# Deformable convolution of one fused kernel: row-tiled spreading of the sample points, 64-row products, three taps a multiply

## The reference, cut to what matters

```
def _dcnv4(t, H, W, Wv, bv, Wom, bom, Wo):     # N=8 images, 16x16 pixels, C=32, G=4 groups of Cg=8, K=9 taps
    value = (t @ Wv + bv).reshape(N, H, W, G, Cg)
    om = (t @ Wom + bom).reshape(N, H, W, G, 3 * K)
    offset = om[..., :2 * K].reshape(N, H, W, G, K, 2)
    mask = om[..., 2 * K:]
    loc_y = ys + ky + offset[..., 1]
    loc_x = xs + kx + offset[..., 0]
    sampled = _bilinear_gather(value, loc_y, loc_x)      # zero outside the image
    out = (sampled * mask[..., None]).sum(axis=4)
    return out.reshape(N, L, C) @ Wo
```

## Time and profile before

| what | value |
|---|---|
| median of three runs | 520.41 us (519.21 to 521.89) |
| the profiled execution | 518.91 us, its span 517.1 us |
| mean granted clock of TensorE | 0.952 of full speed |
| busy: PE / PEld / DVE / ACT / POOL | 463.7 / 325.7 / 419.9 / 302.2 / 212.5 us |
| instructions: PE / DVE / ACT / POOL | 3334 / 998 / 554 / 168 |

### The profile page before, as it was taken

The page is one execution under the profiler, slowest core; times in us unless marked ns, Lnnn a source line. Parts: engine busy times, 40 slices in busy tenths (PEclk is TensorE's granted clock), DMA queues, the critical chain, the costliest instruction groups (busy, mean ns, idle before and its releaser), DMA issues.

```text
span 517.1 us, 10243 instructions
## 1 busy us (share of the span) xinstructions
PE 463.7 (90%) x3334; PEld 325.7 (63%) x3334; DVE 419.9 (81%) x998; ACT 302.2 (58%) x554; POOL 212.5 (41%) x168
## 2 busy tenths in 40 slices
PE   6979889999987759999999859999999899699785
PEld 5868523333346637777778637877777888455474
DVE  4978899998783498999999598999998586799551
ACT  3742448898744347777771277777760223798540
POOL 4004450000000078999984189999974031000000
PEclk9999899999999678999999969999999999899995
DMA  8700000000000000000000000000000000000000
GB/s 325 329 2 0 1 1 1 1 1 0 1 1 1 0 2 1 1 0 0 1 0 1 1 1 1 0 1 0 0 1 0 1 1 1 2 1 2 2 1 20
DMA packets 1475, 9.16 MB, mean 18 GB/s; under 512 B 160, under 2 KB 928, under 8 KB 1056
## 3 DMA queue, kind: packets, MB, share of 16 engines
q1 hardware_dynamic: 1296, 8.62, 4.2%
q10 hardware_dynamic: 144, 0.07, 0.1%
HBM read 8.43 MB, written 0.26 MB: 17 GB/s over the span
## 4 chain that ended last, share of the span: by engine, by line
PE 60%; DVE 20%; ACT 8%; issue 6%; POOL 4%; DMA 0%; DVEq 0%; SPq 0%; POOLq 0%
PE bank L1226 24%; PE bank L1171 13%; PE bank L1207 6%; ACT RINGS L555 3%; DVE RINGS L780 2%; PE bank L985 2%; PE bank L1312 2%; PE bank L1292 2%; PE bank L1176 2%; DVE SMT L859 1%; DVE PRD L850 1%; POOL RINGS L255 1%; POOL PR L276 1%; DVE PR L692 1%; DVE XN L623 1%
## 5 line engine op out<-in xcount | busy, mean ns | idle before, releaser
L1226 PE MATMUL bank<-VB,RINGS 128*128 (+1 forms) x576 | 159.6, 415 | 0.3
L255 POOL TENSOR_TENSOR RINGS<-LXA,cst 128x1152 f32<-128x1152 f32 x32 | 69.2, 2162 | 125.8 <-DVE LXA L831 125.8
L1226 PEld LDWEIGHTS bank<-VB,RINGS 128*128 128x128 f32 x576 | 104.5, 195 | 23.0 <-issue 1.8
L850 DVE TENSOR_TENSOR PRD<-bank,HYM 128x288 f32<-128x288 f32 x288 | 110.6, 448 | 8.4 <-PE bank L1226 3.7
L780 DVE TENSOR_SCALAR RINGS<-XP,wb 128x512 f32<-128x512 f32 x176 | 79.4, 527 | 7.9 <-PE bank L1171 6.6
L460 ACT ACTIVATE RINGS<-XP,wb 128x512 f32<-128x512 f32 x112 | 70.1, 712 | 16.9 <-PE bank L1171 16.8
L985 PE MATMUL bank<-cst 128*128 128x128 f32 x650 | 78.6, 281 | 0.0
L985 PEld LDWEIGHTS bank<-cst 128*128 128x128 f32 x650 | 77.5, 198 | 0.5
L1171 PE MATMUL bank<-RINGS,cst 128*32 128x512 f32 x576 | 74.4, 598 | 3.7 <-DVE RINGS L780 3.7
L324 POOL TENSOR_TENSOR PRD<-PRD 128x864 f32<-128x864 f32 x32 | 65.2, 2038 | 17.5 <-DVE PRD L850 17.5
L859 DVE TENSOR_REDUCE SMT<-PRD 128x1728 f32 (+1 forms) x32 | 62.1, 1941 | 0.1
(11 more groups left out here) (247 smaller groups left out, 519.6 us busy)
## 6 DMA issues: line engine op xcount, KB each, us to landing
wb<-in_wb SPq DMA_DIRECT2D x1, 3068.5 KB, 12.3
wd<-in_wd SPq DMA_DIRECT2D x1, 2729.5 KB, 20.8
wc<-in_wc SPq DMA_DIRECT2D x1, 1255.0 KB, 14.9
cst<-in_cst SPq DMA_DIRECT2D x1, 645.0 KB, 5.4
XC<-in_x SPq DMA_DIRECT2D x2, 128.0 KB, 2.4
out_y<-XC SPq DMA_DIRECT2D x2, 128.0 KB, 1.8
wa<-in_wa SPq DMA_DIRECT2D x1, 209.0 KB, 5.5
cst<-in_cst ACTq DMA_DIRECT2D x1, 66.0 KB, 2.7
```

The costliest lines, as they stand in the source:

```text
L255: pool.tensor_tensor(view(DXY, o, [[WW, KG * NA], [1, WW]]), view(LXA, n * KG * NA, [[1, KG * NA], [0, WW]]), view(cst, CST["xg"], [[0, KG ...
L850: dve.tensor_tensor(view(PRD, (half * K9 + k) * 288, [[72, G], [NR, CG], [1, NR]]), view(bank[2 + (9 * half + k) % LOOK], 0, [[72, G], [NR ...
L1226: pe.matmul(bank[2 + (9 * half + k) % LOOK][:, 0:288], view(HXT, (half * K9 + k) * P, [[1, P]]), view(VB, b * 288, [[1, 288]]), start=True ...
```

## The change

The x hats are no longer made pixel by pixel and then turned. Instead the x locations themselves are turned, once an image (72 locations a pixel, laid out in three groups of 32 columns, 24 of them used: `turn_points`, 2 transposes). ACT copies them out (`points_out`). A matmul with a 0/1 matrix (`select`, a new constant of 384 columns) then repeats each location over 16 partitions: `spread(t)` is three matmuls, each contracting 32 rows at partitions 0, 32 and 64, into banks 4, 5 and 6, 256 columns (both halves) each. ACT takes |location - column| straight from these banks with the column as its bias (a new constant `mx`, one number a partition), three instructions of 256, and then relu(1 - .) on all 768 (`hats`). There are three such groups t an image, of three taps each. The banks are reused from one t to the next.

The y hats: POOL subtracts the rows for both halves (`rows_off`), ACT takes the absolute value and the relu on 648 elements (`rows_hat`), POOL multiplies by the mask (`masked`). HY holds them in place, in two buffers that alternate from image to image.

The products: for a half and three taps, six matmuls. Each contracts 64 rows (two groups) with 144 columns; the pair of one tap takes partitions 0 to 63 and 64 to 127 and writes different banks. DVE multiplies all three taps at once, 864 elements (`sample`); two pairs of banks alternate. POOL's `pairs` adds 864 elements as before, DVE's `sums` reduces 1728 as before. The channels come out in another order, for which the host permutes Wo. All loops over images are written out. Before the loop only image 0's points are finished; those of images 1 to 3 follow before the first multiply, those of images 4 to 7 are put into image 1. In PSUM, one tensor replaces the eight banks, with a small class that gives views.

The core of the diff (the old functions that it removes are in the code above):

```diff
+            def rows_off(turn, b):
+                i = B * turn + b
+                pool.wait_ge(lxa_ready, pointed(turn, b))
+                after(pool, prod_used, 6 * (i - 1))
+                for half in range(2):
+                    ins = pool.tensor_tensor(by_trio(HY, (b % 2 * 2 + half) * HYN), by_point(LY, 2 * b + half),
+                                             view(cst, CST["yg"], [[0, 3], [0, 3 * G], [1, NR]]), ALU.subtract)
+                ins.then_inc(dy_ready, 1)
+            def masked(turn, b):
+                pool.wait_ge(hy_ready, B * turn + b + 1)
...
+                for b in range(B):
+                    if b + 1 < B:
+                        rows_off(turn, b + 1)
+                    pairs(turn, b, 0)
+                    if b + 1 < B:
+                        masked(turn, b + 1)
+                    pairs(turn, b, 1)
...
+            def points_out(i):
+                act.wait_ge(t_done, i + 1)
+                after(act, sel_done, 9 * i)
+                act.activation(view(LXT, 0, [[1, NPIX]], n=LXW), bank[7][0:LXW, 0:NPIX], ACT.Copy).then_inc(lxt_ready, 1)
+            def rows_hat(i):
+                hy = view(HY, i % 2 * 2 * HYN, [[1, 2 * HYN]])
+                act.wait_ge(dy_ready, i + 1)
+                act.activation(hy, hy, ACT.Abs).then_inc(hy_abs, 1)
+                act.wait_ge(hy_abs, i + 1)
+                act.activation(hy, hy, ACT.Relu, scale=-1.0, bias=cv("one", 1)).then_inc(hy_ready, 1)
+            def hats(i, t):
+                after(act, prod_done, 6 * (i - 1))
+                hx = i % 2 * HXN + 3 * t * NPIX
+                for quad in range(3):
+                    act.wait_ge(sel_done, 9 * i + 3 * t + quad + 1)
+                    act.activation(view(HX, hx + quad * NPIX, [[1, NPIX]]), bank[4 + quad][:, 0:NPIX], ACT.Abs,
+                                   bias=cv("mx", 1)).then_inc(abs_done, 1)
+                act.wait_ge(abs_done, 9 * i + 3 * t + 3)
+                act.activation(view(HX, hx, [[1, 3 * NPIX]]), view(HX, hx, [[1, 3 * NPIX]]), ACT.Relu, scale=-1.0,
+                               bias=cv("one", 1)).then_inc(hat_ready, 1)
...
+                for b in range(B):
+                    i = B * turn + b
+                    points_out(i)
+                    rows_hat(i)
+                    for t in range(3):
+                        hats(i, t)
...
+            def sample(i, half, t):
+                q = 6 * i + 3 * half + t
+                dve.wait_ge(hym_ready, i + 1)
+                after(dve, smp_ready, 2 * i + half - 1)
+                after(dve, paired, 2 * i + half - 1)
+                dve.wait_ge(prod_done, q + 1)
+                dve.tensor_tensor(view(PRD, half * PRN + t * TRIO, [[3 * COLS, GP], [6 * NR, CG], [1, 6 * NR]]),
+                                  view(bank[q % 2 * 2], 0, [[512, GP], [6 * NR, CG], [1, 6 * NR]]),
+                                  view(HY, (i % 2 * 2 + half) * HYN + t * 3 * G * NR, [[6 * NR, GP], [0, CG], [1, 6 * NR]]),
+                                  ALU.mult).then_inc(prod_used, 1)
...
+                offsets(turn, 0, 0)
+                offsets(turn, 0, 1)
+                points(0, 1)
...
+                points(1, B4 - 1)
+                for b in range(B):
+                    i = B * turn + b
+                    sample(i, 0, 0)
+                    sample(i, 0, 1)
+                    if b:
+                        sums(i - 1, 1)
+                    sample(i, 0, 2)
+                    sample(i, 1, 0)
+                    sample(i, 1, 1)
+                    sums(i, 0)
+                    if b == 1:
+                        points(B4, B4)
+                    sample(i, 1, 2)
+                sums(B * turn + B - 1, 1)
...
+            def spread(turn, b, t):
+                i = B * turn + b
+                pe.wait_ge(lxt_ready, i + 1)
+                after(pe, abs_done, 9 * i + 3 * t)
+                for quad in range(3):
+                    pe.matmul(bank[4 + quad][:, 0:NPIX], cv("select", P, t * P, 32 * quad, 32),
+                              view(LXT, 0, [[1, NPIX]], 32 * quad, 32), start=True, stop=True).then_inc(sel_done, 1)
+            def products(turn, b, half, t):
+                i = B * turn + b
+                q = 6 * i + 3 * half + t
+                if half == 0:
+                    pe.wait_ge(hat_ready, 3 * i + t + 1)
...
+                after(pe, prod_used, q - 1)
+                for k3 in range(3):
+                    for gp in range(GP):
+                        ins = pe.matmul(view(bank[q % 2 * 2 + gp], k3 * NR, [[3 * NR, 2 * CG], [1, NR]]),
+                                        view(HX, b % 2 * HXN + (3 * t + k3) * NPIX + half * P, [[1, P]], 64 * gp, 64),
+                                        view(VB, b * COLS, [[NR, 2 * CG], [1, NR]], 64 * gp, 64),
+                                        start=True, stop=True, skip_group_check=True)
+                ins.then_inc(prod_done, 1)
...
+                for b in range(B):
+                    ahead = b + 1 < B
+                    if ahead:
+                        turn_points(turn, b + 1)
+                    for u in range(6):
+                        products(turn, b, *divmod(u, 3))
+                        if ahead and u in (0, 2, 4):
+                            spread(turn, b + 1, u // 2)
```

More of the change, by code:

```diff
@@ new lines, in masked, with pairs @@
+            def masked(turn, b):
+                pool.wait_ge(hy_ready, B * turn + b + 1)
+                for half in range(2):
+                    hy = by_trio(HY, (b % 2 * 2 + half) * HYN)
+                    ins = pool.tensor_tensor(hy, hy, by_point(MM, 2 * b + half), ALU.mult)
+                ins.then_inc(hym_ready, 1)
+            def pairs(turn, b, half):
+                i = B * turn + b
+                pool.wait_ge(prod_used, 6 * i + 3 * half + 2)
+                first, second = (view(PRD, half * PRN + t * TRIO, [[1, TRIO]]) for t in range(2))
+                pool.tensor_tensor(second, second, first, ALU.add).then_inc(paired, 1)
@@ L475, in _ @@
             norm(4, "eps6")
-            def absolute(turn, b, half):
-                n = 2 * b + half
-                o = half * HATS
-                act.wait_ge(dxy_ready, 16 * turn + n + 1)
-                act.activation(view(DXY, o, [[1, HATS]]), view(DXY, o, [[1, HATS]]), ACT.Abs).then_inc(abs_done, 1)
-            def hats(turn, b, half, begun=False):
-                n = 2 * b + half
-                o = half * HATS
-                if not begun:
-                    absolute(turn, b, half)
-                act.wait_ge(abs_done, 16 * turn + n + 1)
-                after(act, hx_turned, 3 * (16 * turn + n - 1))
-                after(act, hym_ready, 16 * turn + n - 1)
-                act.activation(view(HXY, o, [[1, HATS]]), view(DXY, o, [[1, HATS]]), ACT.Relu, scale=-1.0,
-                               bias=cv("one", 1)).then_inc(hxy_ready, 1)
@@ L507, in deform @@
                                    view(src, bh * NPIX, [[WW, NR], [7 * WW, NA], [1, WW]]), ACT.Copy).then_inc(xw_ready, 1)
-                hats(turn, 0, 0)
-                absolute(turn, 0, 1)
-                turned(turn, 0, 0)
-                hats(turn, 0, 1, begun=True)
-                def body(b, first=False):
-                    for half in range(2):
-                        if not (first and half == 0):
-                            turned(turn, b, half)
-                        hats(turn, b + 1, half)
-                body(0, first=True)
-                with act.Fori(1, B - 1) as b:
-                    body(b)
-                for half in range(2):
-                    turned(turn, B - 1, half)
+                for b in range(B):
[4 more added lines that the diff above has]
+                        hats(i, t)
                 act.wait_ge(smp_turned, turn + 1)
@@ L861, in sums @@
+            def sums(i, half):
+                bh, b4 = divmod(i % B, B4)
+                dve.wait_ge(prod_used, 6 * i + 3 * half + 3)
+                dve.wait_ge(paired, 2 * i + half + 1)
+                dve.tensor_reduce(view(SMT, bh * NPIX + half * P + b4 * C, [[1, C]]),
+                                  view(PRD, half * PRN + TRIO, [[3 * NR, C], [TRIO, 2], [1, 3 * NR]]), AX.XY,
                                   ALU.add).then_inc(smp_ready, 1)
             def deform(turn):
-                for half in range(2):
-                    offsets(turn, 0, half)
-                    points(half, 2, B4)
+                offsets(turn, 0, 0)
+                offsets(turn, 0, 1)
+                points(0, 1)
@@ L867, in deform @@
                 if turn == 0:
[L868 removed]
+                    dve.wait_ge(vb_clear, 2)
                 values(turn, 0)
[L870 to L872 removed]
                 values(turn, 1)
[L874 to L885 removed]
@@ L1241, in deform @@
                     ins.then_inc(val_done, 1)
-                turn_hats(turn, 0, 0)
-                def body(b, more, first=False):
-                    products(turn, b, 0, True, first)
```

(14 more changed lines are left out.)

237 lines of the change are left out of this document (80 added, 157 removed).

## The result

The changed kernel took 533.55 us (median of 4 runs, 530.22 to 535.55) against 521.07 (519.21 to 521.89, 4 runs) for the kernel before on the same chip: a ratio of 1.024, 95% interval 1.018 to 1.030. The forecast was 527, range 508 to 541, slower at 0.65. The profiled execution took 530.22 with a span of 528.4, and before 518.9 with 517.1: 11.3 us more. From the second copy of XNC to the end of the last reduction the first turn now takes 179.95 to 292.60 = 112.65 us, and the second, from the end of YC on, 110.93, where they took 106.1 and 106.2. That is 6.5 + 4.7 = 11.2 us, so all but 0.1 us of the difference lies in the two deformable turns.

What follows compares the result with a forecast made beforehand. PE bound the old loop, DVE hardly behind; a ring of waits would bind the new. A turn: 14.1 + 8 x 11.0 + 4.0 + 1.0 + 2.4 (clock) = 109.5, +3.4; two turns +6.8, so 525.7 profiled, 527 median, range 508 to 541.

Steps and rivals of the forecast that it cites:

- The ring: Deformable loop: waits from one image's last multiply through POOL, ACT, PE and DVE to the next image's, 11.0 us.
- Tile shape: PE, between spreads, products and transposes: each change of tile shape adds 0.09 us.
- rival 4: PE array empties at each tile-shape change: 0.17 at two changes in the ring, 0.34 an image, 532 us; chance 0.10.
- hand-overs between engines: In the ring: six passes from one engine to the next, about 0.05 us each, 0.3 together.
- 64-row tiles: Products on PE: pairs run side by side, 6 rounds of 144 columns at 0.122, 0.73 us a trio.
- Rival 3: Products on PE: 64-row tiles don't run side by side, a trio stays at 1.46 us, kernel 541; chance 0.08.
- Start of a turn: From XNC to the first product: 12.3 us at full clock, 14.1 with PE at 1.2 GHz, against 17.0 before.
- Points of images 4 to 7: Now between two multiplies of image 1: taken as 4.0 us a turn.
- The clock in the loop: PE clock falls in two images of eight, +1.2 us each, +2.4 a turn; bounds none to 14 us.
- the last reduction: End of a turn on DVE: 1.0 us added to the turn's sum.
- Rival 2: The ring stands but PE's clock holds in the loop: 522 us, 519 if also at the start; chance 0.26.
- Rival 1: Loop: ring hidden, DVE sets the pace, 9.6 + 0.3 us an image, a turn 98.3, kernel 505; chance 0.12.

Runs made afterwards that it cites:

- g3_shapes: e3_spread_later with the matmuls without a reader in a turn's tail replaced by 128-row, 32-row and alternating ones; 519.68 us in its only execution.
- k3_pool_adds_warm: g4_pool_adds plus 18 matmuls without a reader in the points' gap and three small ones in each image; 506.30 us, ratio 0.972 to the kernel before.
- e3_spread_later: The changed kernel with each spread put one product trio later on PE; 512.25 us, ratio 0.986 to the kernel before the change.
- g1_warm_ends: e3_spread_later plus matmuls without a reader behind a turn's first two spreads and in its last image; 504.85 us, ratio 0.968 to the kernel before.
- g4_pool_adds: e3_spread_later, third HY buffer, g1_warm_ends' matmuls; POOL adds one half's third trio, DVE reduces 864 elements there; 508.73 us, ratio 0.977 to the kernel before.

## Why the prediction was right, and which terms were off

**The ring: right, 0.11 short.** It was put at 11.0 us and measures 11.11. Multiply 1.06 (measured 1.05), distances 0.74 + 0.79 (1.46 for two), y hats to the first absolute value 1.53 (364.99 to 366.50, 1.51), three absolute values 1.21 (1.19), reduction 1.94: all within 0.07. The cause was put to the test on three engines, and each edit took it away.

**Tile shape: mechanism misread, effect small.** I took 0.09 a change and gave rival 4 a chance of 0.10. The timeline of PE in the kernel after shows more:

```profile
240.19 0.71 PE L1209 MATMUL bank<-RINGS,cst 32*128 32x256 f32 x6
240.83 1.01 PE L1224 MATMUL bank<-VB,RINGS 64*128 64x144 f32 x12
241.76 0.42 PE L1200 MATMUL bank<-cst,LXA 128*96 128x128 f32 x2
```

Two rounds of the spread are 0.43, but the next shape starts 0.64 after it; six product rounds are 0.73, and the transposes start 0.93 after: 0.2 us each, the same as in g3_shapes. The array empties before another shape starts, as the Trainium skill says (TensorEngine Tiling (Array Packing), Key Properties), and the trace agrees. My reading of the earlier trace rows was the error. A record of a matmul there starts before the one ahead of it ends, but I took that for work side by side; its own length holds the wait. In the ring one change counts, and 0.2 in place of 0.09 is 0.11 or so, as much as 11.11 exceeds 11.0 by. (The hand-overs between engines also came to some 0.45 in place of 0.3, and the shorter distances, y hats and absolute values made up for it.) Rival 4 had the mechanism, but it counted two changes in the ring at 0.17 more each, where the runs show one at 0.11 more.

**64-row tiles: right.** The records of a pair start 7 ns apart and the rounds of one trio 0.122, so six rounds are 0.73. Rival 3 is out.

**Start of a turn: right.** 14.1 forecast, 13.97 and 14.0 measured, with the clock down from 188.8 us on. In the timeline of PE the second spread still takes 0.71 us; the third and the first trio run at 1.2 GHz:

```profile
188.19 0.71 PE L1209 MATMUL bank<-RINGS,cst 32*128 32x256 f32 x6 [1.97 <-ACT RINGS L505]
190.24 1.23 PE L1209 MATMUL bank<-RINGS,cst 32*128 32x256 f32 x6 [1.35 <-ACT RINGS L505]
...
191.99 1.81 PE L1224 MATMUL bank<-VB,RINGS 64*128 64x144 f32 x12
```

**Points of images 4 to 7: right sum, wrong parts.** 4.0 forecast, 15.03 - 11.11 = 3.92 measured. DVE's five instructions hold the multiply up for only 2.11 us (217.10 to 219.21; 211.59 to 213.70 above), since POOL has nothing to do from 217.42 on; the 4.9 us of before had POOL at work beside them, as in k3_pool_adds_warm. The other 1.8 are the clock, at 1.2 GHz for 6.8 us of that image.

**The clock in the loop: the term that was mis-sized.** I took two images of eight. Beside the period with the points in each turn, which had a fall both times, five of six periods of the first turn and three of six of the second had one, ten of 14 in all. What they cost over 11.11 in those six is 4.5 us in the first turn and 2.6 in the second, against 2.4 in my sum. I also put the last reduction at 1.0 and it takes 1.99. The sum for the first turn: -0.1 (start) + 0.2 (eight images, the last at 10.26) - 0.1 (points) + 2.1 (clock) + 1.0 (reduction) = 3.1, and 109.5 + 3.1 = 112.6; for the second 1.4, and 110.9. The profile's 525.7 so becomes 530.2, as measured. The median lies 3.3 above the profiled execution, the fastest of its four.

What made two images too few: I compared the emptiest stretch of the loop with two stretches elsewhere and found it nearer to the one that fell, and then didn't follow that through. The Trainium skill (TensorE: Matmul & The Clock Gate, A second HAM failure mode) says that brief idling between groups of matmuls makes the clock oscillate; the trace agrees. In the loop of the kernel after PE idles 2.2 to 2.4 us ahead of the second spread of an image twelve times, and ten of these twelve gaps have a fall of the clock in them or within 2 us behind them. Here it fell at 250.2 us:

```profile
248.76 0.71 PE L1209 MATMUL bank<-RINGS,cst 32*128 32x256 f32 x6 [2.36 <-ACT RINGS L505]
```

That the gap is the cause is likely and not shown by this alone. With the gap cut to 1.02 us (e3_spread_later) five of 14 periods had a fall, two of them in the last image, which has no spreads. Rival 2, which trusted that it would hold, is out.

**Rival 1** gave 505 us if POOL and ACT ran about 1.4 us ahead. They didn't in this kernel. g1_warm_ends, in which the ring is open, takes 504.9, but that it is the same number is luck: its images take 10.26 rather than 9.9, and its start isn't held up by the clock as the 14.1 of that sum is.

## What to carry to other kernels

When an edit takes the bounding engine off the bound, don't add up engines: walk one turn of the loop through every buffer that is written again, and count the other engines' steps on that walk. Here the ring was opened by moving one step with no work removed (each spread of 0.43 us by one place: nearly 4% of the kernel's time). Walk the loop again after each such edit: with work moved to POOL, the next ring ran through POOL. And an engine whose clock follows its load turns each wait into a second loss, so price the emptier PE image by image, and put matmuls without a reader only where the trace shows the gap ahead of a fall.

## What the runs showed of the hardware

- A change between 128-, 64- and 32-row shapes costs 0.19 to 0.21 us of PE for these float32 matmuls, either way.
- Two 64-row tiles with 144 columns ran side by side at 0.12 us a pair; the starts lay 7 ns apart.
- The clock fell ten times in the two loops of the kernel after, where PE never idled more than 2.4 us at a time. It fell more often where DVE was made faster (g4_pool_adds, mean granted clock 0.921 to 0.951 in five executions, against 0.961 to 0.964 in the four of g1_warm_ends).
- Matmuls without a reader before the first product kept the clock at 2.4 GHz; the same kind of matmuls added once it had fallen left it at 1.2 GHz for longer, 17.1 us against 10.2. Why wasn't settled: the trace shows PE fully busy in that time.
- A multiply of 864 elements out of PSUM took 1.053 us and the next started 0.97 after it, where three of 288 took 3 x 0.365 from start to start: joining them saved 0.12 us a trio.
- The same DVE instruction on 288 elements took 0.31 us with POOL idle and 2.01 us with a POOL sum running beside it (g1_warm_ends and k3_pool_adds_warm).
